# A convolution with attention on one core: the main filter split in three, one home for the input

## What is computed

```python
x = x + conv_ref(_ln_c(x), gamma, beta, qkv_w, qkv_b, proj_w, proj_b)
# conv_ref:
qkv = conv1d_same(group_norm(xf, gn_gamma, gn_beta), qkv_w, qkv_b)      # 256 -> 768 channels, 16 taps
h = qkv_attention(qkv.reshape(b * NUM_HEADS, -1, t)).reshape(b, -1, t)   # 4 heads of 64
return (xf + conv1d_same(h, proj_w, proj_b)).reshape(b, c, *spatial)     # 256 -> 256, 5 taps
t = _to_tokens(x); t = t + _L0_ffn_ref(_ln_t(t))                         # digits, per position
```

## Time and profile before

| | |
|---|---|
| median of three runs | 1106.17 us |
| the profiled execution | 1104.99 us, its span 1103.2 us |
| busy share | PE 90%, DVE 65%, ACT 59%, POOL 21% |
| mean granted clock of PE | 0.965 |
| first matmul of a filter | 26.4 us |
| first score matmul of step 1 | 162.8 us |
| steps 1 to 7, each up to the next step's start | 105.7, 105.6, 106.4, 127.2, 105.5, 105.5, 105.7 us |

### The profile page before, as it was taken

How to read it: one execution, slowest core, us unless ns; L and a number is a source line. 1 busy time by engine, 2 the same in 40 slices (tenths; PEclk the granted TensorE clock), 3 DMA queues, 4 the chain that set the end, 5 groups by cost and what they waited for, 6 DMA issues and landing times.

```text
span 1103.2 us, 18112 instructions
## 1 busy us (share of the span) xinstructions
PE 987.4 (90%) x7250; PEld 684.0 (62%) x7250; DVE 716.3 (65%) x1222; ACT 650.2 (59%) x1049; POOL 233.4 (21%) x164
## 2 busy tenths in 40 slices
PE   2888649999999999999598999999999999988864
PEld 1555526667766776667366666766677668766654
DVE  5988557654775577668466555465536665777767
ACT  4673617664676477767565565465636575665532
POOL 2736122100330132124050000010001004313320
PEclk9998879999999999999799999999999999999987
DMA  7050033593459357737644284537445873453522
GB/s 272 13 180 1 1 125 65 99 212 68 91 111 247 51 118 168 165 67 146 171 77 86 47 185 106 87 63 182 93 67 110 201 167 73 97 124 59 115 58 77
DMA packets 284515, 122.59 MB, mean 111 GB/s; under 512 B 268304, under 2 KB 270736, under 8 KB 283536
## 3 DMA queue, kind: packets, MB, share of 16 engines
q1 hardware_dynamic: 284432, 121.44, 49.5%
HBM read 34.24 MB, written 15.87 MB: 45 GB/s over the span
## 4 chain that ended last, share of the span: by engine, by line
PE 59%; DVE 11%; ACT 8%; issue 7%; DMA 2%; POOL 1%; SPq 0%; ACTq 0%; POOLq 0%; DVEq 0%
PE cM L1049 15%; PE cQ L1049 14%; PE cP L1049 13%; PE psT L1118 4%; PE psV L1095 4%; PE psS L1118 4%; PE psV L1099 3%; ACT arena L909 2%; DVE smx L1495 2%; DVE W L1280 1%; DMA arena<-arena 1%; DVE arena L1472 1%; PE cM L990 1%; ACT arena L921 1%; PE cP L990 1%
## 5 line engine op out<-in xcount | busy, mean ns | idle before, releaser
L1049 PE MATMUL cP<-U,W 128*128 128x256 f16 (+1 forms) x1536 | 224.3, 303 | 13.8 <-DVE W L1280 12.5
L1049 PE MATMUL cM<-U,W 128*128 128x256 f16 (+1 forms) x1536 | 223.3, 301 | 11.4 <-DVE U L1309 7.4
L1049 PE MATMUL cQ<-U,W 128*128 128x256 f16 (+1 forms) x1536 | 225.6, 302 | 5.7 <-DVE W L1280 3.5
L1049 PEld LDWEIGHTS cP<-U,W 128*128 128x128 f16 x1536 | 150.7, 98 | 82.0 <-issue 11.6
L1049 PEld LDWEIGHTS cM<-U,W 128*128 128x128 f16 x1536 | 149.6, 98 | 81.1 <-issue 8.9
L1049 PEld LDWEIGHTS cQ<-U,W 128*128 128x128 f16 x1536 | 149.7, 98 | 74.2 <-issue 6.0
L1472 DVE SCALAR_TENSOR_TENSOR arena<-arena,smx 128x1024 f16<-128x1024 f32 x128 | 178.5, 1394 | 1.3 <-ACT arena L921 0.6
L902 ACT ACTIVATE smx<-smx,esc 128x1 f32<-128x1 f32 x128 | 37.5, 293 | 207.4 <-DVE smx L1495 207.0
L921 ACT ACTIVATE arena<-arena,smx 128x1024 f16<-128x1024 f32 x128 | 147.0, 1148 | 4.2
L1495 DVE TENSOR_REDUCE smx<-psS 128x1 f32<-128x1024 f32 x64 | 77.9, 1217 | 71.5 <-PE psS L1118 71.1
L1495 DVE TENSOR_REDUCE smx<-psT 128x1 f32<-128x1024 f32 x64 | 78.0, 1219 | 57.1 <-PE psT L1118 56.7
(11 more groups left out here) (212 smaller groups left out, 1202.1 us busy)
## 6 DMA issues: line engine op xcount, KB each, us to landing
staging<-w_qkv SPq DMA_DIRECT2D x20, 512.0 KB, 5.1
kept_u<-U SPq DMA_DIRECT2D x4, 2077.0 KB, 10.0
U<-kept_u SPq DMA_DIRECT2D x16, 519.2 KB, 4.4
arena<-x_tok SPq DMA_DIRECT2D x8, 512.0 KB, 6.4
arena<-arena SPq DMA_DIRECT2D x16, 256.0 KB, 3.8
W<-x_tok SPq DMA_DIRECT2D x4, 1024.0 KB, 6.1
out_tok<-W SPq DMA_DIRECT2D x3, 1024.0 KB, 4.3
kept_h<-arena SPq DMA_DIRECT2D x4, 514.0 KB, 4.2
```

Source lines behind the costliest of these rows:

```text
L1049: last = mm(out, W[:, j, wl, c, wat + tap, :], U[:, slot, ul, c, at:at + width], start=(c == 0 and tap == 0 and wl + ul == 0), stop=(c == ...
```

## The change

The main filter is split in three filters of 4 taps too. A tile has five groups: 0 holds the two outer thirds of the main filter, 1 its common third (256 columns), 2 the common thirds of the two difference filters, 3 and 4 the other thirds. Each group is again in one of three banks. POOL has 10 sums of weights per tile instead of 8, two of them sums of sums (parts 4 and 5), and a new operation that joins the two common outputs (`join_common`). ACT writes the main copy straight into y and has a new copy of 256 columns (`main_common_copy`).

U has one home of 2340 KB in six parts. Batch 0 is built there. Batches 1 to 3 are built part by part in `temp_a` (260 KB) and `temp_b` (520 KB), each part is stored (`store_u`) and the home is reloaded in four pieces for every step from 1 on (`load_u`). Squares and scales of tiles 5, 4 and 3 are made in step 2. The residual stage keeps its buffers in W alone.

```diff
-            1: {1: [("first", 2)], 2: [("fine", 2, 0)], 3: [("fine", 2, 1)], 6: [("fine", 2, 2)], 7: [("fine", 2, 3)]},
+            1: {3: [("u", 2, 0), ("u", 2, 1)], 6: [("u", 2, 2)], 8: [("u", 2, 3), ("u", 2, 4)], 10: [("u", 2, 5)],
+                14: [("u", 3, 0), ("u", 3, 1)], 17: [("u", 3, 2)]},
...
+            def store_u(b, part):
+
+                wide = part in (0, 4, 5)
+                lo, hi = u_at(part)
+                sp.wait_ge(S["ulo_done"], SPLITS * b + part + 1)
+                sp.dma_start(kept_u[b][:, lo:hi], u_home(b, part)[:, :, :, :].rearrange("p l c w -> p (l c w)")) \
+                    .then_inc(S["ub_out" if wide else "ua_out"], 16)
...
+                sp.wait_ge(S["conv_done"], GROUPS * (TILES * n - 1) + (1, 3, 4, 5)[q])
+                lo, hi = ((0, UB), (UB, UB + 3 * UA), u_at(4), u_at(5))[q]
+                sp.dma_start(U[:, lo:hi], kept_u[n % NB][:, lo:hi]).then_inc(S[f"u_in{q}"], 16)
...
+            BATCH_2 = {3: 0, 4: 1, 6: 2, 8: 3, 9: 4}
+            BATCH_3 = {14: 0, 15: 1}
...
+                    if k == 0 and u in BATCH_2:
+                        store_u(2, BATCH_2[u])
+                    if k == 0 and u == 10:
+                        store_u(2, 5)
                         load_eo()
...
+            def u_high(b, part):
...
+                if b >= 2 or (b == 1 and part > 1):
+                    wait(act, "ub_out" if wide else "ua_out",
+                         16 * (FAMILIES * (b - 1) + (max(part - 3, 0) if wide else part - 1)))
+                a(u_part(u, part, 0), u_source(b, part), ACT.Copy).then_inc(S["uhi_done"], 1)
...
-            ITEMS = [[(0, 0, t) for t in (0, 2, 4, 6)], [(0, 1, t) for t in (0, 2, 4)], [(0, 1, 6), (1, 0, 0), (1, 1, 0)],
-                     [(1, 0, 1), (1, 1, 1), (2, 0, 1), (2, 1, 1)], [(2, 0, 2), (2, 1, 2), (3, 0, 1)],
-                     [(3, 1, 1), (3, 0, 2), (3, 1, 2)]]
+            ITEMS = [[(0, 0, 1), (0, 0, 2), (0, 1, 1)], [(0, 1, 2), (1, 0, 0), (1, 1, 0)], [(2, 0, 0), (2, 1, 0), (2, 0, 1)],
+                     [(2, 1, 1), (3, 0, 1), (3, 0, 2)], [(3, 1, 1), (3, 1, 2), (4, 0, 1)], [(4, 0, 2), (4, 1, 1), (4, 1, 2)]]
...
-                    if conv and i in (13, 14):
-                        qk_lo(3 * n + 1, 0, i - 13)
+                    if conv and i == 13:
+                        qk_lo(3 * n + 1, 0, 0)
+                        qk_lo(3 * n + 1, 0, 1)
```

More of the change, by code:

```diff
@@ L149, in build, with u_at, u_view, u_home @@
         BATCH_AT = (0, 1, 3, 2)
-        def u_home(b):
-            return U[:, (b + 1) % 2]
+        def u_at(part):
+            wide = part in (0, 4, 5)
+            at = (0, UB, UB + UA, UB + 2 * UA, UB + 3 * UA, 2 * UB + 3 * UA)[part]
+            return at, at + (UB if wide else UA)
+        def u_view(part):
+            lo, hi = u_at(part)
+            return U[:, lo:hi].rearrange("p (l c w) -> p l c w", l=2, c=CT)
+        U_B = [u_view(part) for part in (0, 4, 5)]
+        U_A = [u_view(part) for part in (1, 2, 3)]
+        def u_home(b, part):
+            if b == 0:
+                return u_view(part)
+            return temp_b if part in (0, 4, 5) else temp_a
         def wst(m):
@@ L546, in extra @@
                     sums(k, tile)
-                if kind == "first":
-                    first_low(k)
-                if kind == "fine":
-                    fine_low(k, tile)
+                if kind == "u":
+                    u_low(k, tile)
                 if kind == "ring":
@@ L1037, in conv_item @@
-                pe.wait_ge(S["wlo_done"], place(m, part))
-                if g == 0:
-                    out, taps, wat, uat, width = bank_of(j, 0)[:, :], range(t, t + 2), 0, 0, HALF
-                else:
-                    third = 0 if g == 1 else t
-                    half = t if g == 1 else t - 1
-                    out = bank_of(j, g)[:, QUART * half:QUART * (half + 1)]
-                    kind = 3 * d + third
-                    taps, wat, uat, width = range(QTAPS), PH_TAPS + QTAPS * kind, fine(d, third), QUART
@@ L1048, in conv_item @@
+                half = (t - 1, 0, t, t - 1, t - 1)[g]
+                out = bank_of(j, g)[:, QUART * half:QUART * (half + 1)]
+                u, at = (U_A[family], 0) if third == 0 else (U_B[family], QW * (third - 1))
+                for tap in range(QTAPS):
                     for wl, ul in ((0, 0), (0, 1), (1, 0)):
-                        last = mm(out, W[:, j, wl, c, wat + tap, :], U[:, slot, ul, c, at:at + width],
-                                  start=(c == 0 and tap == 0 and wl + ul == 0),
-                                  stop=(c == 1 and tap == (PH_TAPS if g == 0 else QTAPS) - 1 and wl == 1),
+                        last = mm(out, W[:, j, wl, c, QTAPS * (3 * family + third) + tap, :], u[:, ul, c, at + tap:at + tap + QUART],
+                                  start=((g, c, t) in OPENERS and tap == 0 and wl + ul == 0),
+                                  stop=((g, c, t) in CLOSERS and tap == QTAPS - 1 and wl == 1),
```

671 lines of the change are left out of this document (349 added, 322 removed), and 24 rows, old and new, of tables (ACT_BEFORE, DVE_AT, POOL_AT).

## The result

The changed kernel is slower: 1136.95 us median of 4 runs (1135.47 to 1137.79) against 1106.7 of the kernel before (4 runs, 1106.09 to 1107.38). The ratio is 1.0278, 95% interval 1.0266 to 1.0291. The forecast was 1086 us, range 1044 to 1108. Its profiled execution took 1135.47 us, span 1133.6.

The account below looks back on a forecast made before the run. The prediction took PE to bound the kernel, busy in all of 105.6 us in steps 2 and 6. 1104.99 - 52.7 - 21.6 + 4 + 7 + 36 + 7 = 1084.7, plus 1.2 for the median: 1086 us, range 1044 to 1108.

Parts of the forecast that it names:

- part 2: Tiles 3 to 5 scaled in step 2: step 4 loses its waits, -21.6 us; added work in steps 3 and 4, +4 us.
- rival B: Steps 1 to 7: main copy and bank reuse come late, up to +3 us each, 1107 us at most; chance 0.10.
- Part 1: Filter matmuls, steps 1 to 7: 72 of 256 columns replace 48 of 512, 7.53 us less per step, -52.7 us.
- Rival D: Filter matmuls: 72 short ones cost more than 48 long ones, 1139 us at break-even; chance below 0.01.
- Part 3: Step 0: extra DVE and POOL work and a new ACT wait, less a PE wait; +7 us, bounds -3 and +16.
- the wait for the copy: Step 0: PE's 3.94 us wait for a copy behind a 2 MB store; now 0.5 MB stand ahead of it.
- Parts 4 and 5: Steps 1 and 2: ACT waits for stores and loads, +36 us; PE's slow clock after five such waits, +7 us.
- The laps of the stores: Steps 1 and 2: ACT waits for temp_a or temp_b until a store queued behind SP's transposes lands; 8, 8, 8 and 7 us.
- The 7 us for the clock: Steps 1 and 2: matmuls run slow after PE idles, 1.5 us per wait, five waits; bounds 0 and +12.
- a tight bank in slot 14: Steps 5 to 7: main copy must free its bank in time; counted at nothing, +3 us per step as upper end.
- A: Steps 1 and 2: ACT gets its stores in time and waits are hidden; 1035 to 1062 us, chance 0.24.
- C: Steps 1 and 2: store laps feed each other, slower from 63 us of waits and slow clock; 1118 us, chance 0.13.

Follow-up runs that it names:

- e_fewmm: Changed kernel with only one of three products of each filter tap in steps 1 to 7; 1105.55 us.
- e_tinylo: e_ring3 with the low halves of the weights of tiles 3 to 5 made on only 16 columns of one tap; 1108.43 us.
- e_s0tiny: Changed kernel with the six new sums of sums of tiles 0 to 2 made on only 16 columns of one tap; 1133.25 us.
- e_s0parts: e_s0tiny with the high and low halves of the same six parts also made on only 16 columns of one tap; 1129.95 us.
- e_poolstore: Changed kernel with the stores of batches 2 and 3 issued by POOL behind the low half, not from SP's queue; 1111.25 us.
- e_nosq: Changed kernel with squares of tiles 3 to 5 taken of 128 columns only and without the weight loads for them in step 2; 1123.38 us.
- e_order_pws: Changed kernel with high and low halves later in steps 3 and 4, and the projection's scale ahead of heads_low in step 7; 1134.96 us.
- b_fewmm: Kernel before the change with only one of three products of each filter tap in steps 1 to 7; 1029.45 us.
- e_ring3: Changed kernel with a third buffer for the tap sums of tiles 3 to 5; 1129.41 us.

## Why the prediction was wrong

**The step that failed is the end of part 2: "+4 us (bounds 0 and +12)" for steps 3 and 4.** Over 98.05 us they took 20.1 and 18.0 more, 38.1 in sum, three times the upper bound. I had priced the added work (10 sums a tile, 25 parts in step 3) as if the loop of attention behind it had room down to PE's new pace. It hadn't: with two thirds of PE's filter products gone, step 3 still takes 118.2 us (e_fewmm). In the kernel before the same cut leaves 102.6 us, of which some 4 belong to the scale that the change moved away. So at most 4.5 us of the miss were there before any part was added, and perhaps none. The added parts and the scales of three tiles raised DVE's busy time in step 3 from 74.34 us (below, step 3 of the kernel before, columns as in the earlier trace rows) to 86.23. A low half of 512 columns took 0.86 us there, not the 0.75 of the sum.

```profile
373.25:479.67 106.42, 105.91 (x780) 71.46 (x779) 74.34 (x97) 76.45 (x120) 28.11 (x18) 1.00 0.60 129
```

e_tinylo shows that most of it is DVE's time: 21.8 of the 38.1 us go with the low halves. In a slot the maximum on DVE releases the exponential on ACT, this the reciprocal on DVE, and the weights' low halves stand between that and the next maximum; I read the order of these three off the program, the runs show only that the work on DVE counts and the work on ACT doesn't. The two buffers of sums, which the profile names (34.9 us of waits), are worth about 7 us. The other 9 us I did not take apart. Part of it may be rival B in small: the longest single wait of PE in step 3 was 5.4 us for a bank that ACT had not copied yet, and in step 4 it was 3.3 us (who for whom, us in total, times, longest). No run takes these waits away alone.

```profile
PE cP L1110 <- ACT y_all L871: 5.4, 1, 5.4
```

I had the rows for it. Step 4 of the kernel before is DVE-heavy, and I read its 127.2 us as 105.6 plus a stall because PE's time was 105.6. "PE is busy in all of the step" says that nothing else was longer than PE; it does not say by how much.

**Part 1, matmuls: right.** Steps 5 and 6 took 98.05 us with PE busy throughout (forecast 98.1), 7.5 us less than before; the pace is 109.6 ns as measured before. Rival D falls with it. The 131 ns for 512 columns that the Trainium skill gives ("TensorE: Matmul & The Clock Gate", "Back-to-back issue gap") are shown by no run here; the trace has 216.7. But only steps 5 and 6 got the full gain, 15 of 52.7 us.

**Part 2, scales in step 2.** The waits of step 4 for them did go: PE's longest wait of that step is the 3.3 us for a bank. Step 4 is 11.1 us shorter, where it was to be 27.

**Part 3, step 0: mis-sized.** +16.8 us against +7 (upper bound +16). Up to the transposes that end step 0 it was even 21.0 (156.86, now 177.83); the wait for the copy behind them, which fell, gave 4.2 back. The term that I counted at nothing is POOL's: e_s0tiny gives 5.2 us for the six sums. Of the 7.7 us for DVE, e_s0parts shows 3.4 for the halves. The first filter matmul comes 4.2 us later (26.44, now 30.67): it waits for DVE's low half of a part of 1040 columns, which stands behind two fine differences and an ACT copy of the same part. 1.2 of these 4.2 us are within the 8.5 of the two runs (5.2 and 3.4). The remaining 9.5 us (21.0 - 8.5 - 3.0) I did not take apart. DVE's differences of 518 columns may be in it: up to the first scores they took 1.05 us each on average before (8 of them), and 1.44 now (12).

The wait for the copy went as forecast. PE's first score matmul had nothing to wait for:

```profile
179.56 1.53 PE L1176 MATMUL psS<-arena 128*128 128x512 f16 x4
```

**Parts 4 and 5, laps and clock: the place right, the sum partly luck.** Steps 1 and 2 lost 42.8 us against what the shorter filter alone would have given (+27.7, and 15.1 for two steps of 7.53); the forecast was 36 + 7 = 43. The places were the named ones: ACT's rounding for a DMA 37.5 us (some 30 forecast), the squares 12.2. But the terms came out otherwise. The laps of the stores were to cost 31 us, and e_poolstore gives 24.8 back. The squares were to cost 5, and e_nosq takes 14.9 off step 2. The 7 us for the clock no run shows: with two thirds of PE's filter work gone step 2 still took 127.1 of its 128.4 us, so a slow PE can hardly have set its length. Errors of opposite sign met in the sum. The split between the steps was off by 6 us either way, more in step 2. That the queues were full when a transpose held SP for 5.69 us is my reading; no run shows it.

**Step 7: overlooked.** I looked for a tight bank in slot 14 and weighed only the main copy. The opener of group 2 of the last tile waits for the projection's scale. Group 2 now opens with the first item of slot 14, where it opened with the third of slot 15, and DVE brings the scale behind q and k: 4.83 us of idle, the step 6.8 longer than its neighbours, 5.4 of which e_order_pws gives back.

**The rivals.** A, that all waits are hidden, fell with step 2. B, late banks in every step, fell with steps 5 and 6. C had the sign and not the cause: what steps 1 and 2 lost, 42.8 us, stayed below the 63 from which C decides. Whether the laps fed each other no run shows. Its +12 for steps 3 and 4 was its nearest term, and too small by 26. None of my cases had the right one: that in the steps with the most preparation DVE's work would set the length, far above PE's new pace.

## What to carry to other kernels

Before a change that makes the busiest engine faster, ask for each stage what its length would be without that engine; a cut of its work in both kernels (b_fewmm, e_fewmm) gives an upper bound in one run each. Then look in that run for waits that the change will move or make: the 102.6 us of step 3 held one of 11.5 us. A gain per step counts only where this floor lies below the new pace; where it doesn't, work added to the engine of the loop lengthens the step. And take a store that somebody waits for out of a queue of instructions that wait for others: the landing took 3.3 us, the waits up to 10.6.

## What the runs showed of the hardware

A long wait in a view need not be a price. ACT's 34.9 us behind the sums fell to 7.6 with a third buffer, and to 9.3 by another order; the steps gave back 7 us in the first case and nothing in the second, since ACT then idled for DVE's maximum instead.

A store issued by POOL landed about as fast as one by SP (3.1 and 3.3 us for 520 KB, 2.8 and 2.6 us for 260 KB), and took 0.58 us of POOL's queue to issue, after 0.41 us of waiting for its own low half (e_poolstore, in order of time):

```profile
208.78 0.58 POOL L569 DMA_DIRECT2D kept_u<-temp_a  x1 [0.41 <-POOL temp_a L565]
```

The stores stand in steps 1 and 2 alone, and both steps got shorter (by 7.0 and 17.9 us), so what they took of POOL's time cost less than it brought.

The granted clock went with PE's idle time and not with DVE's load in these rows: 0.97 in step 3 of e_ring3, 1.00 in the same step of e_tinylo, where PE idled for 6 instead of 13 us, and 0.78 in e_fewmm, where it idled for 51 us. At 0.78, and with a third of the filter products, step 3 was as long as at 0.97 with all of them.
